# A transformer layer on one core: eight weight copies queued later, and one copy of turned values ahead of the exponentials

## The reference

```
x = x + attention(layernorm(x))      # 16 heads of 16, rotary positions
x = x + ffn(layernorm(x))

attention: q, k, v = x @ qkv_w.T; q, k rotated
           scores = q k / 4, masked: a key is seen if it isn't later and is
           within 128, in the same block of 64, or one of the first 4
           softmax, times v, times out_w.T
ffn:       h = silu(x w1 * s1) * (x w2 * s2)            # 256 -> 1024
           h = gelu(h h1 * s)                            # 1024 -> 1024
           h = gelu(h h2 * s)                            # 1024 -> 1024
           out = h w3 * s3                               # 1024 -> 256
```

## Time and profile before

| | |
|---|---|
| runs | 1084.67, 1086.20, 1086.23 us; median 1086.20 |
| profiled execution | 1084.15 us, span 1082.3 us |
| PE busy | 1050.4 us (97%) |
| ACT busy | 718.1 us (66%) |
| DVE busy | 643.6 us (59%) |
| POOL busy | 450.8 us (42%) |
| share of PE in the chain that ended last | 79% |
| DMA | 190.16 MB, mean 176 GB/s |
| mean granted clock of TensorE | 0.992 |

### The profile page before, as it was taken

One profiled execution on the slowest core, in us unless ns is written; L12 is line 12 of the kernel. 1 busy time (PEld: TensorE's weight loads), 2 busy tenths in 40 slices (PEclk: granted clock), 3 DMA queues, 4 the chain that ended last, 5 costly groups with the idle time before them and its releaser, 6 DMA issues.

```text
span 1082.3 us, 21614 instructions
## 1 busy us (share of the span) xinstructions
PE 1050.4 (97%) x7602; PEld 878.4 (81%) x7602; DVE 643.6 (59%) x1988; ACT 718.1 (66%) x1776; POOL 450.8 (42%) x622
## 2 busy tenths in 40 slices
PE   6869999999999999999999999999999999999998
PEld 3547878898788977889778897889878898889887
DVE  5865576556765568556675566655576555556322
ACT  3966676955958658667586576785676955966422
POOL 5642463433624418235263254542463431532433
PEclk9889999999999999999999999999999999999999
DMA  8788569455565356555483654736556365432540
GB/s 317 288 281 247 172 206 307 127 180 176 193 180 156 122 188 228 147 156 175 135 264 107 195 166 136 244 98 196 175 166 189 109 181 179 123 109 76 179 136 21
DMA packets 112797, 190.16 MB, mean 176 GB/s; under 512 B 7216, under 2 KB 66864, under 8 KB 111664
## 3 DMA queue, kind: packets, MB, share of 16 engines
q1 hardware_dynamic: 112256, 182.45, 54.2%
q10 hardware_dynamic: 432, 6.29, 1.4%
HBM read 150.97 MB, written 45.09 MB: 181 GB/s over the span
## 4 chain that ended last, share of the span: by engine, by line
PE 79%; ACT 9%; DVE 5%; POOL 3%; issue 2%; DMA 1%; SPq 0%; ACTq 0%; POOLq 0%; DVEq 0%
PE bank L791 35%; PE bank L761 11%; PE bank L818 5%; PE bank L562 5%; PE bank L693 5%; ACT Sm L974 4%; PE bank L629 4%; PE bank L659 3%; PE bank L667 3%; DVE Sm L1177 2%; PE bank L593 2%; ACT L994 2%; PE bank L720 1%; POOL b_lo L1469 1%; PE bank L704 1%
## 5 line engine op out<-in xcount | busy, mean ns | idle before, releaser
L974 ACT ACTIVATE Sm<-Sm,smin 128x260 f32<-128x260 f32 (+2 forms) x512 | 241.3, 473 | 154.2 <-DVE smin L1177 153.7
L791 PE MATMUL bank<-b_hi,W 128*128 128x512 f32 x512 | 209.3, 409 | 0.0
L791 PE MATMUL bank<-a_hi,W 128*128 128x512 f32 x512 | 206.5, 403 | 0.1
L791 PE MATMUL bank<-b_lo,W 128*128 128x512 f32 x512 | 201.1, 393 | 0.0
L791 PE MATMUL bank<-a_lo,W 128*128 128x512 f32 x512 | 200.8, 392 | 0.0
L761 PE MATMUL bank<-x_hi,W 128*128 128x256 f32 x512 | 125.0, 286 | 0.0
L761 PE MATMUL bank<-x_lo,W 128*128 128x256 f32 x512 | 123.4, 283 | 0.0
L1478 POOL TENSOR_TENSOR a_lo<-a_act,a_hi 128x256 fp32r<-128x256 f32 x128 | 94.4, 741 | 61.8 <-ACT a_hi L1025 61.7
L1177 DVE CUSTOM_DVE_ANT_0 Sm<-bank,msk,gmin 128x256 f32<-128x256 f32 x256 | 108.2, 478 | 9.3 <-PE bank L629 7.0
L791 PEld LDWEIGHTS bank<-a_hi,W 128*128 128x128 f32 x512 | 96.4, 188 | 17.5 <-DVE a_act L1260 0.3
L791 PEld LDWEIGHTS bank<-a_lo,W 128*128 128x128 f32 x512 | 96.5, 188 | 17.0
(11 more groups left out here) (136 smaller groups left out, 2197.7 us busy)
## 6 DMA issues: line engine op xcount, KB each, us to landing
W<-w_scratch SPq DMA_DIRECT2D x168, 512.0 KB, 4.1
qk_scratch<-split SPq DMA_DIRECT2D x56, 512.0 KB, 4.1
Qs<-qk_scratch SPq DMA_DIRECT2D x112, 128.0 KB, 4.4
Ks<-qk_scratch SPq DMA_DIRECT2D x14, 1024.0 KB, 8.9
w_scratch<-in_ffn_w SPq DMA_DIRECT2D x22, 512.0 KB, 7.0
x_in<-in_x SPq DMA_DIRECT2D x8, 512.0 KB, 7.3
stage_a<-in_ffn_w ACTq DMA_DIRECT2D x2, 2048.0 KB, 9.5
x<-in_x SPq DMA_DIRECT2D x8, 512.0 KB, 3.9
```

The lines of the kernel that those rows point to most:

```text
L791: mm = nc.tensor.matmul(bank[n % 2][:, :], lhsT.bitcast(F32) if general else lhsT, rhs, start=(kk == 0 and part == 0), stop=(kk == NH - 1 ...
L974: ex = nc.scalar.activation(row, row, ACT.Exp, bias=smin[:, r, c:c + 1], scale=-1.0, accum_out=rowsum[:, i % 2, col:col + 1])
```

## The change

Two edits. In the opening SP issues the first eight copies of weights in step 13, behind `save_split` of the last part of batch 1, and no longer in step 8. In the rounds with an ffn, `keep_prev` in step n = NH = 8 stands ahead of the exponentials of unit 8 and no longer behind them.

```diff
--- before.py
+++ after.py
@@ -467,10 +467,10 @@
                         if n == 8 and r + 3 < NB:
                             load_x(r + 3)
                     if r == -1:
-
                         if n in (9, 11, 12, 13):
                             save_split(1, n // 12, int(n in (11, 13)))
-                        if n == 8:
+                        if n == 13:
+
                             for m in OTHERS[:EARLY]:
                                 save_weights(m)
                         if n == 12:
@@ -1051,6 +1051,8 @@
                     if with_a:
                         if n == 14:
                             keep_globals(a, 0)
+                        if with_f and n == NH:
+                            keep_prev(a, n - T_LAG)
                         if n < UNITS:
                             exponentials(a, n)
                         if r == -1 and n == 0:
@@ -1059,7 +1061,7 @@
                             keep_xnT(r, 1)
                         if with_f and n % NH == 6 and n < 2 * NH:
                             gelu(r, n // NH, 1)
-                        if GROUPS <= n - T_LAG < UNITS:
+                        if GROUPS <= n - T_LAG < UNITS and not (with_f and n == NH):
                             keep_prev(a, n - T_LAG)
                         if n == UNITS:
                             keep_x2hi(a, 0)
```

## The result

The changed kernel takes 1076.4 us (median of 4 runs, 1075.92 to 1076.90), where the kernel before, run beside it, takes 1086.2 us (4 runs, 1084.67 to 1086.71). The ratio is 0.9912, with a 95% interval of 0.9895 to 0.9928. Forecast were 1076.6 us and a range of 1073.0 to 1082.5.

A forecast was written before the change was run, and what follows sets the result against it. PE bounds the kernel, busy 1050.4 of 1082.3 us, waiting in the opening and in rounds 0 to 6. Gains of 5.1 + 3.5 = 8.6 us, taken from the middle of two bases, gave 1076.6 us, range 1073.0 to 1082.5.

The forecast's parts named there:

- The 7.60 us wait goes and one of 2.5 us comes: Opening: ACT's 7.60 us wait for the q stores before `split<-q` goes; it waits 2.5 us before `split<-k` instead.
- The pair that ran undisturbed: Two stores issued at 70.8 and 71.3 on a nearly empty SP queue; their 4.9 us priced the moved-up stores' trip.
- The second part starts 5.1 us earlier: Opening: ACT's k part with f = 0 starts at 67.3 instead of 72.44, when its own stores have landed.
- The opening gains 5.1 us: PE follows ACT's chain up to the gated part: 5.1 us gained, range 1.6 to 7.6, nothing counted for the clock.
- A late queue costs nothing: Round 0: first W load lands at 120.2, wanted at 120.9, hidden by 0.7 us; upper end, PE stands 5.6 us.
- rival 1: Weights come late in round 0: PE stands up to 5.6 us, 3.0 us of gain stay, 1082.2 us; chance 0.13.
- Rival 2: All fourteen copies take 3.0 us each, PE stands 13.2 us at the third deep tile: 1090 us; chance 0.06.
- The condition on the price of a copy: At 2.7 us a copy on SP's queue, PE's stall in round 0 and the gain were to be about equal.
- The copy ahead of the exponentials, 3.5 us: Rounds 0 to 6: PE's stall before line 667's transposes goes, 0.50 us a round, 3.5 us for seven; range 0 to 5.2.
- Rival 3: The moved copy brings nothing, another PE wait in the round takes back 0.5 us: gain 5.1, 1080.1 us; chance 0.09.
- Rival 4: Opening: ACT waits for the k stores instead, with a trip of 8.4 us: gain 1.6 + 3.5, 1080.1 us; chance 0.06.
- The base: Starting time for the sum: profiled execution 1084.15 us gives 1075.55, median 1086.20 gives 1077.6; the middle was taken.

The follow-up runs named there:

- the repeat: The changed kernel run once more, unaltered, beside the kernel before: 1076.4 us, ratio 0.9913; its profile is the second one of the changed kernel.
- experiment 3: Changed kernel with 29 transposes filling PE's idle time in the opening: 1076.3 us (bank 7), 1074.5 us (bank 6); with k made earlier and 27 transposes, 1075.6 and 1075.3 us.
- experiment 4: Changed kernel with eight more 512 KB copies behind the moved ones: 1092.1 us; with four more: 1084.1 us; with the eight copies in step 11 instead: 1076.9 us.

## Why the prediction was right

It was right in its direction, its mechanisms and nearly its sum; some terms were off and offset each other. That the time came within 0.2 us of 1076.6 is partly luck: openings with the same instructions differ by up to 1.3 us, and the timed runs of the changed kernel by 1.0 us here and 2.3 us in the repeat.

- **The 7.60 us wait goes and one of 2.5 us comes.** Right: 2.39 us. The pair that ran undisturbed was the right row to take: the data were there at 62.00, the part started at 66.87, 4.87 us later, for the 4.9 us forecast.
- **The second part starts 5.1 us earlier.** 5.57 us, of which 0.38 us were there already: DVE began the lower part of k at 61.03, not at 61.41. So 5.2 us come from the change, and as many in the second profile (17.53 us from DVE's start on q's lower part to `split<-k` before, 12.29 there).
- **The opening gains 5.1 us.** 4.51 us in the first profile, of which 0.37 us lie ahead of the edits, so 4.14; by the same mark 5.14 us in the second, and 5.40 with the copies alone. The sum took nothing for the clock, and this is the term that was mis-sized: it moves the gain by over 1 us from one execution to the next. The clock fell as allowed for, but I priced it only for line 646 (0.9 us) and as the same in both kernels. In the changed kernel's first profile the slow stretch lay later and covered lines 659 to 693 too, whose products DVE waits for; that is 0.86 us between the two exponentials above (5.37 - 4.51). With the clock held (experiment 3) the opening gains 6.55 us. The Trainium skill, "TensorE: Matmul & The Clock Gate", section "HAM oscillation — how this bites in real kernels", says that a gap in which PE waits for data lowers the clock of what follows. The traces agree, and for gaps of 1.11 and 2.73 us too, which I had left open.
- **A late queue costs nothing.** Right. By my sum the first W load lands at 120.2, and PE would have stood after 0.7 us of delay. It landed 5.0 us before it was wanted in the first profile and 2.3 us before in the second. The second follows the sum closely: SP came to the copies at 73.70 (73.9 in the sum), the loads went out at 114.10 (114.8), and the first took 4.9 us (5.4), against a copy to y_acc of 7.5 us (6.3) and copies at 1.67 us each (13.37 / 8) for 2.0. In the first, SP came at 71.85, as DVE's lower parts were earlier too, the loads went out at 112.46, right behind PE's last gated tile, and the first took 4.0 us. The earlier trace rows has the median of eleven loads, while line 418 at 117.0 in the trace of before, the same load, had landed in 3.7. Four added copies cost a wait of 4.4 us, so rival 1 exists; it starts at 2.6 to 4.9 us more of delay in SP's queue. For the eight copies that is 2.0 to 2.3 us each ((13.37 + 2.6) / 8 and (13.74 + 4.85) / 8), where the sum had 2.1 (2.0 + 0.7 / 8).
- **Rival 2, slower,** is the same place with more delay. Eight added copies show it: at 1092.1 us that kernel is slower than the one before. The condition on the price of a copy (2.7 us or more) wasn't near: in no profile did the eight, issued behind the stores, take over 14.6 us, 1.8 each. That their first price, 22.45 us, came from the stage loads ahead, was argued from the code. The trace of before fits it: 11.47 of the 22.45 us are the issue of the third copy alone, from 40.08 to 51.55, and the last stage load (line 495) landed at 49.7. That the price is gone at the new place is measured. The Trainium skill, "DMA: Bandwidth & Descriptors", section "Issuing engines are not separate DMA queues", says that all DMAs run on the same 16 engines and interleave, whoever starts them. The traces agree: a k store with the copies right behind it landed 0.5 us later (experiment 4), and four copies more made PE wait 4.4 us for a load behind them.
- **The copy ahead of the exponentials, 3.5 us.** Right: 3.59 us. Rounds 0 to 5 took 129.36 for 129.92 us (0.56 each) and round 6 gave 0.26. Rival 3 falls with the moved copy alone: it has the whole 3.6 us.
- **Rival 4, the wait only moves,** falls with the 4.87 us from data to start.
- **The base.** The spans differ by 8.1 us, the medians by 9.8. The profile of before lies 2.05 us under its median, that of the changed kernel 0.4. Taking the middle of both bases gave 1076.6; from the median alone it would have been 1077.6. So against the medians the gain was underrated by 1.2 us (8.6 for 9.8), and against the profiles overrated by 0.5.

## What to carry to other kernels

Where one engine issues all DMAs, order its queue by who waits: bulk that nobody awaits goes behind the small stores, and the price is read where the first awaited load behind it lands, from that load's own row and not from a median, and from more than one profile: the margin here was 5.0 us in one and 2.3 in the next. A wait that ends shortens the gap, but PE may still fall to half clock; price every product in the slow stretch that others wait for, or give PE something harmless to do in the gap. And a short copy that frees a bank belongs ahead of long work on its engine, but not ahead of its own input by even half a microsecond. To compare openings, take a mark ahead of the edit, or differences from elsewhere are read as its gain.

## What the runs showed of the hardware

- **The moment at which the clock falls varies between executions of one program.** The same opening took 40.88, 40.95, 41.14 and 42.14 us from a mark ahead of the edits to round 0, with clocks that fell at different times, and 39.62 and 39.64 us with the clock held. The first four timed runs of the changed kernel come in two pairs: spans of 1074.1 and 1074.2 us with a mean clock of 0.996, and 1075.1 twice with 0.994.
- **Idle time filled with 29 transposes** (some 3.6 us of PE's time: 0.98 + 2.57) kept the clock at 1.00 in both profiles and made the opening 1.2 to 2.5 us shorter.
- **A last store of 128 KB** landed 1.7 to 1.9 us after its issue in ten profiles and 3.3 to 4.0 us in four (filled transposes; these with the k part earlier, twice; four extra copies). It is on the path to the end, so it can hide or feign a gain of 2 us.
- **Copies of 512 KB from DRAM to DRAM** held the issuing queue for 1.7 us each when little was in flight, 1.9 us for eight more behind them, and 2.8 us at the old place.
- **After a wait of 4.4 us,** PE's clock fell only once the work had begun again: two matmuls at 0.47 and 0.42 us, then 0.63 us each for over 2 us. After one of 10.0 us the very first took 0.77 us, and the granted clock had fallen within the wait (0.50 from 131 to 133 us).
